# Expert tiles: gate and up computed transposed, with weight blocks stationary and 128 tokens streamed

## What is computed

```
x_flat = x.reshape(B * S, D)                                   # D = 256
router_probs = softmax(x_flat @ gate_w)                        # 8 experts
top_k_probs, top_k_idx = top_k(router_probs, 2)                # normalised to sum 1
gate_up = einsum('nd,edh->enh', x_flat, gate_up_w)             # h = 2 * 512
hidden = silu(gate_up[..., :512]) * gate_up[..., 512:]
expert_out = einsum('enf,efd->end', hidden, down_w)            # 512 -> 256
output = sum over the two chosen experts of prob * expert_out
```

## Time and profile before

| | |
|---|---|
| median of three runs | 2418.78 us |
| span of the profiled execution | 2410.7 us |
| median less this span | 8.1 us |
| mean granted TensorE clock | 0.955 |
| PE busy over the span | 2081.0 us (86%) |
| PEld busy | 1058.4 us (44%) |
| DVE busy | 1571.5 us (65%) |
| ACT busy | 1210.0 us (50%) |
| POOL busy | 911.2 us (38%) |

### The profile page before, as it was taken

One profiled execution on the slowest core, in us unless ns is written; L12 is line 12 of the kernel. 1 busy time (PEld: TensorE's weight loads), 2 busy tenths in 40 slices (PEclk: granted clock), 3 DMA queues, 4 the chain that ended last, 5 costly groups with the idle time before them and its releaser, 6 DMA issues. The chain is left out here.

```text
span 2410.7 us, 46759 instructions
## 1 busy us (share of the span) xinstructions
PE 2081.0 (86%) x11964; PEld 1058.4 (44%) x12049; DVE 1571.5 (65%) x4036; ACT 1210.0 (50%) x2360; POOL 911.2 (38%) x894
## 2 busy tenths in 40 slices
PE   4889999999898898998998988861099999999997
PEld 2433444444343444443444433321066666666665
DVE  3477888887887887887888898841633333333332
ACT  1256566566565565665656666640444444444443
POOL 2222242332423423333234244133245555555554
PEclk9899999999999999999999998985599999999999
DMA  2322332322222323223232232201523333333332
GB/s 99 83 74 53 86 87 69 93 71 81 85 71 68 87 69 88 77 70 87 69 78 82 65 85 74 64 27 45 191 45 57 53 56 54 53 56 52 55 54 37
DMA packets 181071, 171.97 MB, mean 71 GB/s; under 512 B 40002, under 2 KB 169620, under 8 KB 180884
## 3 DMA queue, kind: packets, MB, share of 16 engines
q1 hardware_dynamic: 150612, 134.94, 20.1%
q0 software_dynamic: 30272, 34.80, 9.1%
HBM read 100.82 MB, written 68.93 MB: 70 GB/s over the span
## 5 line engine op out<-in xcount | busy, mean ns | idle before, releaser
L1147 DVE TENSOR_REDUCE mxs<-bank 128x1 f32<-128x512 f32 x1024 | 697.1, 685 | 205.0 <-PE bank L493 186.5
L823 ACT ACTIVATE pt<-bank 128x512 f32<-128x512 f32 x1024 | 588.5, 593 | 388.8 <-PE bank L502 369.3
L493 PE MATMUL bank<-ks,qs 96*128 96x512 bf16 x1024 | 397.9, 390 | 84.1 <-DVE mxs L1147 53.3
L502 PE MATMUL bank<-qs,ks 99*128 99x512 bf16 x1024 | 393.4, 385 | 9.2 <-ACT pt L823 8.7
L1697 POOL DMA_INDIRECT out<-y_sb,ids x136 | 214.6, 1578 | 273.3 <-DMA out<-y_sb,ids 193.7
L511 PE MATMUL bank<-pt,v_sb 128*32 128x512 f32 x2048 | 278.0, 615 | 0.0
L493 PEld LDWEIGHTS bank<-ks,qs 96*128 96x128 bf16 x1024 | 103.1, 101 | 357.5 <-DVE mxs L1147 214.0
L1826 DVE TENSOR_TENSOR hl<-bank,hh 128x512 bf16<-128x512 f32 x136 | 94.1, 692 | 210.7 <-ACT hh L1796 210.7
L1822 DVE TENSOR_TENSOR hid_e<-bank,act_g 128x512 f32<-128x512 f32 x136 | 94.1, 692 | 210.5 <-PE bank L1743 209.0
L974 POOL DMA_INDIRECT list_dram<-pay,slot_i x130 | 138.3, 1064 | 240.9 <-DVE pay L1272 206.7
L1743 PE MATMUL bank<-gu_l,xh 128*128 x544 | 206.9, 380 | 22.9 <-issue 21.2
(11 more groups left out here) (283 smaller groups left out, 3529.2 us busy)
## 6 DMA issues: line engine op xcount, KB each, us to landing
qs<-qk_dram SPq DMA_DIRECT2D x128, 128.0 KB, 2.6
ks<-qk_dram SPq DMA_DIRECT2D x64, 192.0 KB, 3.4
xt<-x_t SPq DMA_DIRECT2D x16, 512.0 KB, 4.2
h_dram<-h_sb SPq DMA_DIRECT2D x16, 512.0 KB
qs<-qk_dram SPq DMA_DIRECT2D x128, 64.0 KB, 2.2
ks<-qk_dram SPq DMA_DIRECT2D x64, 128.0 KB, 3.4
hw<-h_dram SPq DMA_DIRECT2D x16, 512.0 KB, 4.3
out<-hw SPq DMA_DIRECT2D x16, 512.0 KB, 2.9
```

Source lines behind the costliest of these rows:

```text
L493: mm(score[u % 2][:, :], qs[0:QK, h, blk(t)], ks[0:QK, h, :], start=True, stop=True) \
L502: mm(scoret[u % 2][:, :], ks[0:QK + MROWS, h, blk(t)], qs[0:QK + MROWS, h, :], start=True, stop=True).then_inc(s("pe_st"), 1)
L823: f(pt[:, t % 2, j, :], scoret[u % 2][:, :], ACT.Exp).then_inc(s("act_exp"), 1)
L1147: v.reduce_max(mxs[:, t, g * GH + j:g * GH + j + 1], score[u % 2][:, :], AX.X).then_inc(s("dve_mx"), 1)
```

## The change

Gate and up are computed the other way round: a block of 128 by 128 weights is stationary and the tile's 128 rows of x are streamed, so the result has the hidden features on the partitions, four blocks of 128 beside one another in the same bank. There are 48 matmuls of 128 columns where there were 12 of 512. The four transposes of the hidden values and their bank go; the hidden values get two buffers and ACT and DVE split them where DVE wrote them. On ACT that split now stands ahead of the scaled result of the tile before.

```diff
-    hid = sb("hid_e", [128, F])
+    hid = sb("hid_e", [128, 2, F])
...
             for bank, lo, done in ((gate_b, 0, pe_g), (up_b, F, pe_u)):
-                m = 0
-                for c in range(DC):
-                    for a, w in ((xh, gu[0]), (xh, gu[1]), (xl, gu[0])):
-                        m += 1
-                        last = mm(bank[k][:, :], a[:, k, c, :], w[:, bass.ds(e, 1), c, lo:lo + F],
-                                  start=(m == 1), stop=(m == 3 * DC))
+                for f in range(FC):
+                    m = 0
+                    for c in range(DC):
+                        for a, w in ((xh, gu[0]), (xl, gu[0]), (xh, gu[1])):
+                            m += 1
+                            last = mm(bank[k][:, blk(f)], w[:, bass.ds(e, 1), c, lo + f * 128:lo + (f + 1) * 128],
+                                      a[:, k, c, :], start=(m == 1), stop=(m == 3 * DC))
                 last.then_inc(done, 1)
...
-            upto(pe, dve_hid, i.v + 1)
-            upto(pe, act_hh, i.v)
-            upto(pe, dve_hl, i.v)
-            for c in range(FC):
-                last = nc.tensor.transpose(ht_b[:, blk(c)], hid[:, blk(c)], ident[:, :])
-            last.then_inc(pe_ht, 1)
...
+            upto(act, dve_hid, i.v + 1)
+            upto(act, pe_y, i.v - 1)
+            f(hh[:, i.place(2), :, :], hid[:, i.place(2), :].rearrange("p (c n) -> p c n", c=FC), ACT.Copy).then_inc(act_hh, 1)
             if has(i.next(-1), n):
                 take_y(i.next(-1))
-            upto(act, pe_ht, i.v + 1)
-            upto(act, pe_y, i.v - 1)
-            f(hh[:, i.place(2), :, :], ht_b[:, :].rearrange("p (c n) -> p c n", c=FC), ACT.Copy).then_inc(act_hh, 1)
...
-            upto(dve, pe_ht, i.v)
-            v.tensor_tensor(hid[:, :], up_b[i.place(2)][:, :], act_g[:, :], ALU.mult).then_inc(dve_hid, 1)
+            upto(dve, act_hh, i.v - 1)
+            upto(dve, dve_hl, i.v - 1)
+            v.tensor_tensor(hid[:, i.place(2), :], up_b[i.place(2)][:, :], act_g[:, :], ALU.mult).then_inc(dve_hid, 1)
...
-            v.tensor_tensor(hl[:, i.place(2), :, :], ht_b[:, :].rearrange("p (c n) -> p c n", c=FC),
+            v.tensor_tensor(hl[:, i.place(2), :, :], hid[:, i.place(2), :].rearrange("p (c n) -> p c n", c=FC),
                             hh[:, i.place(2), :, :], ALU.subtract).then_inc(dve_hl, 1)
```

More of the change, by code:

```diff
@@ L1627, in expert_phase @@
     pe_g, pe_u, act_silu, dve_hid = sem("pe_g"), sem("pe_u"), sem("act_silu"), sem("dve_hid_e")
-    pe_ht, act_hh, dve_hl, pe_y, act_y = sem("pe_ht"), sem("act_hh"), sem("dve_hl"), sem("pe_y_e"), sem("act_y")
+    act_hh, dve_hl, pe_y, act_y = sem("act_hh"), sem("dve_hl"), sem("pe_y_e"), sem("act_y")
     added, id_set, held = sem("added"), sem("id_set"), sem("held")
     gate_b, up_b = banks[0:2], banks[2:4]
-    xt_b, ht_b, y_b = banks[4], banks[5], banks[6]
+    xt_b, y_b = banks[4], banks[6]
     block = ctx.enter_context(nc.Block())
```

## The result

The changed kernel takes 2687.36 us, the median of 4 runs (2683.76 to 2689.14), against 2418.66 us before (2418.39 to 2422.41): 1.1109 times as long, 95% interval 1.1092 to 1.1126. The prediction said 2687.0 us in a range of 2635 to 2730, with the issue of PE's program as the cause.

What follows compares the result with a forecast made beforehand. PE was taken to bound the kernel, after the change by issue of its program: 6.78 us a tile against 4.785, times 134 +267, with the first tile +268 us; 2418.8 + 268 = 2687 us, range 2635 to 2730.

Steps and rivals of the forecast that it cites:

- the sum: PE's program for one tile: 3.84 + 0.88 + 0.96 + 1.10 = 6.78 us, against 4.785 before; times 134 tiles, +267 us.
- 16 groups at 0.24: Gate and up: 16 groups of three matmuls a tile, each 0.24 us to issue, 3.84 us in all.
- Around down: Row transposes to down's first load 0.88 us, down's four groups 0.96, end of down's issue to next gate 1.10.
- the bounds: Uncertainty of the issue terms; for the 1.10 us before the next gate, 27 us go if its extra passage is worth 0.2.
- First tile and tail: First tile at clock 0.50: 1 us more at most; tail after the last gate: nothing on balance.
- Cover and the other engines: ACT, DVE and POOL have time to spare in a 6.78 us tile; without cover, at most a few tenths of a us.
- Issue that doesn't bind: Rival: PE takes groups at the speed of their columns, tile 4.49 us, 40 us shorter, 2379 us; chance 0.06.
- Weight loads in line: Rival: gate and up's 48 weight loads at 0.10 us queue with matmuls, tile 6.56 us, +237 us, 2656; chance 0.06.
- The clock: Rival: PE, waiting in every group, falls to 1.2 GHz; tile 8.17 us, +453 us, 2872 us; chance 0.05.
- What a register address in the load itself costs: Gate and up's weight loads: taken as nothing; one more step of 0.09 us a group would be +193 us.

Runs made afterwards that it cites:

- the fixed expert: The changed kernel with gate and up always reading expert 0's weights at a fixed address, without their register instructions: 2409.89 us, 0.9993 of before.

## Why the prediction was right

**What bounds the kernel.** Right for PE: issue of register instructions, in the kernel after. For the kernel before it was half the picture. PE's tile (4.66 us) and the chain of additions (4.7) stood within 0.1 us of each other, and I read the 193.7 us of the earlier trace rows only as slack that a longer tile would swallow. It did so here; for any faster tile it is the bound. I also read the 0.17 us of "issue" in the earlier trace rows as a gap of PE. It is mostly a missing record: the chain goes on at 2110.59 with 11 matmuls of L1743 where a tile has 12, and the page counts 477 of the first one's kind where the other two have 544 and 543. No term of the sum rests on it.

**16 groups at 0.24.** From the first load of gate to the row transposes, 2200.49 - 2196.59 = 3.90 us were measured against 3.84. That two instructions of 46 and 32 ns cost 0.24 is shown by taking them out (the fixed expert), putting others in their place (two single ones), and fusing them. The profile's 46 and 32 ns are no price: together they are 0.08 of 0.246 us. Nor does it take a change between matmuls and register instructions. Where such instructions stand in a row in the changed kernel, ahead of down, a TENSOR_LOAD of 299 ns starts at 2200.57, a FUSED_REGOPS of 151 at 2200.93, a SEQ_ASSERT of 18 at 2201.14 and the next at 2201.22: each stands 0.06 us further from the next than it lasts. By this estimate the two of a group come to 0.08 + 2 x 0.06 = 0.20 us. The Trainium skill, Perfetto Trace Analysis, section "Sequencer-only Instruction (DRAIN, etc)", says that the profiler records the execution of such an instruction alone, and not fetch, decode or the push behind it. The trace agrees as far as it goes, with those 0.06 us that no row records; which step takes them no run here shows.

**Around down.** From the row transposes' load to down's first, 2201.42 - 2200.49 = 0.93 against 0.88. By the starts just given, that is 0.36 us for the load of the number, 0.29 for its registers and check, 0.11 for the wait and 0.10 for the first address. From there to the next gate, 2203.34 - 2201.42 = 1.92 against 0.96 + 1.10 = 2.06. The estimate was too long by 0.14. The register instructions of down's four groups go from 2201.32 to 2202.30, 0.98 us against 0.96, but the first 0.10 of them lies ahead of down's first load and is in the 0.93 already. The rest, 2203.34 - 2202.30 = 1.04 against 1.10, was taken from a row in which PE first had a wait to end and transposes to issue, as the bounds said.

**The sum.** 6.78 us was the cycle inside the loop, and 6.75 is what these rows give. But the mean over 134 tiles is 6.850. What the sum lacked is the turn of the loop, once every eight tiles, seen in the chain of waits of the changed kernel:

```profile
2230.40 4.01 PE bank L1744 x48
...
2237.70 4.00 PE bank L1744 x48
...
2244.64 4.02 PE bank L1744 x48
...
2292.51 4.00 PE bank L1744 x48
```

The tile that crosses the turn takes 7.30 us and the next 6.94; eight tiles take 2292.51 - 2237.70 = 54.81, 6.85 each. Before had the turn too, inside its 4.785: from its first weight load of gate to the next tile's, the tile at the turn mostly takes 5.14 to 5.19 us and the others 4.65 to 4.75, so some 0.45 us a turn. I had put what its tiles lose mostly down to rows that came late; nearly half of what they lose over 4.65 is the turn. So the increase is 277 us where the sum said 268, 3% short. That the times agree to 0.01% is luck. I took the 8.1 us between span and median as what lies around the span. The changed kernel's profiled execution took 2689.14 us with a span of 2687.3, and in the 32 later runs of before, too, time and span lie 1.8 to 1.9 us apart. The other 6 were the distance of before's profiled execution from its median. They, and a profiled execution after that lies 1.8 us above its median, nearly made up for the 9 us that the sum lacked.

**First tile and tail.** Small, as said. The first tile streamed at clock 0.50 (the 1.2 GHz level). From its first weight load to the second tile's first matmul it took 1750.29 - 1743.32 = 6.97 us against 1751.34 - 1744.89 = 6.45, so 0.5 more where I had 1 at most. The end, from the last gate, is 2687.3 - 2668.25 = 19.05 us against 18.13, so 0.9 more where I had nothing. In the spans this does not show, because the first gate load came 1.57 us earlier in this execution.

**Cover and the other engines.** DVE, ACT and POOL wait for PE, as predicted. The one new wait on them, ACT's for the hidden product, adds up to 5.5 us over the phase, and the chain of waits does not pass through it.

**The rivals.** Issue that doesn't bind is refuted by all of it. Its price was wrong as well: I gave 2379 us if issue cost nothing, and with no register instruction in gate and up the kernel takes what before takes, since additions stop it at 4.7 us a tile. Without that stop PE's tile is 4.65 in the mean (4.48 inside the loop), of which gate and up take 2.84 us and not 2.74. Weight loads in line: refuted, 0.059 us each at full clock. The clock: it stayed at 1.00 from the second tile to the last (1749.20 to 2680 us) with a gap in every group, so that rival never began. What a register address in the load itself costs, which I left open up to +193 us: nothing that shows, since two register instructions without one gave the same 0.24 us a group, and with one register instruction a group the loads keep their register addresses and gate and up take 2.85 us.

Left open: whether the additions could be set less strictly in order. Two of them side by side could add to one token's row at the same time, where tiles of different experts meet; no run shows what comes of that.

## What to carry to other kernels

Count an engine's instructions that the profile prints as nothing, above all address arithmetic with run-time indices: a matmul that streams for less time than its share of them takes to issue is bound by issue, however busy the array looks. Splitting 512 columns into 128 multiplies that work by four; computing a group's addresses in one instruction, or loading the index once, takes it back. And before paying for a faster engine, look for a second chain that already runs at the same pace: here it left a third of a per cent to be had.

## What the runs showed of the hardware that was not expected

- A register instruction of 32 to 46 ns in PE's program costs about 0.1 us of issue: such instructions stand some 0.06 us further apart than they last. A group with a single fused one of 55 ns, which forms both addresses, is issued in at most 0.14 us, a group with two in 0.246.
- To load an index at run time and check it costs PE's program about 0.65 us (0.36 and 0.29), of which 0.47 are recorded.
- 48 matmuls of 128 by 128 by 128 in bfloat16, each with fresh weights, take 2.84 us, 0.059 each, so the 0.10 us of a weight load hides beside its neighbours.
- A scattered addition is issued in 1.58 us and lands after 3.8; a scattered plain write of the same rows in 1.01 and 2.5.
